# Moving small VectorE steps to GpSimd and ScalarE, and cutting the expert layer's inner units into blocks of 128, in a four-batch transformer kernel

## The reference, cut to what matters

```
x = x + tanh(g_xattn[0]) * L0_xattn(layernorm(x), ctx)    # autocorrelation attention by DFT
x = x + tanh(g_ffn[0])   * L0_ffn(layernorm(x))           # product-key memory
x = x + tanh(g_xattn[1]) * L1_xattn(layernorm(x), ctx)    # 16-head cross attention with rotary positions
x = x + tanh(g_ffn[1])   * L1_ffn(layernorm(x))           # 8 experts, routed
```

```
sx, ix = top_k(sim[0], 8);  sy, iy = top_k(sim[1], 8)
scores, pk = top_k(sx[..., :, None] + sy[..., None, :], 8)
h = softmax(scores) * gelu(x . down_embed[indices]);  out = sum(h * up_embed[indices])
```

```
for e in range(8):
    g = x @ gate_w[e].T ; u = x @ up_w[e].T          # 336 units
    y = (silu(g) * u) @ down_w[e].T ; out += scores[..., e] * y
```

## Time and profile before

| | us |
|---|---|
| median of 3 runs | 481.78 (481.11 to 484.6) |
| the profiled execution's own time | 483.82 |
| its span in the trace | 482.0 |
| PE busy / DVE busy / ACT busy / POOL busy | 393.0 / 331.5 / 202.2 / 124.6 |

### The profile page before, as it was taken

The page is one execution under the profiler, slowest core; times in us unless marked ns, Lnnn a source line. Parts: engine busy times, 40 slices in busy tenths (PEclk is TensorE's granted clock), DMA queues, the critical chain, the costliest instruction groups (busy, mean ns, idle before and its releaser), DMA issues. The chain is left out here.

```text
span 482.0 us, 8024 instructions
## 1 busy us (share of the span) xinstructions
PE 393.0 (82%) x2812; PEld 294.1 (61%) x2812; DVE 331.5 (69%) x1261; ACT 202.2 (42%) x435; POOL 124.6 (26%) x218
## 2 busy tenths in 40 slices
PE   8977699915525358786899899899999999999995
PEld 3866664305514235565576686678877675777784
DVE  7887557999999999989697838798522733132411
ACT  2343532711201004511374714247646387747542
POOL 2000101131023300220232255331242331352653
PEclk9989897975575655775695989999999999999999
DMA  7920000040000000000000000000000000000000
GB/s 221 413 105 0 1 1 2 1 114 1 1 1 1 1 0 1 2 0 2 0 1 2 2 0 1 1 0 13 1 1 2 0 2 13 1 0 1 11 2 12
DMA packets 5613, 11.29 MB, mean 23 GB/s; under 512 B 2004, under 2 KB 4180, under 8 KB 5077
## 3 DMA queue, kind: packets, MB, share of 16 engines
q1 hardware_dynamic: 5572, 10.79, 6.5%
HBM read 10.26 MB, written 0.52 MB: 22 GB/s over the span
## 5 line engine op out<-in xcount | busy, mean ns | idle before, releaser
L413 ACT ACTIVATE Sb<-ps 112x256 f32<-112x256 f32 (+2 forms) x90 | 40.3, 451 | 90.5 <-PE ps L1107 62.2
L384 POOL TENSOR_TENSOR Sb<-Sb 112x256 f32<-112x256 f32 x64 | 50.1, 789 | 108.3 <-ACT Sb L619 106.8
L1079 DVE SCALAR_TENSOR_TENSOR xnb<-ps,score,xnb 128x128 f32<-128x128 f32 x56 | 17.0, 346 | 64.3 <-PE ps L1107 64.1
L1107 PE MATMUL ps<-Y,Xb 128*128 128x32 f16 x512 | 40.0, 249 | 18.6 <-DVE Xb L937 14.7
L1107 PEld LDWEIGHTS ps<-Y,Xb 128*128 128x128 f16 x512 | 37.0, 164 | 26.6 <-DVE Xb L937 16.3
L1107 PEld LDWEIGHTS ps<-dnb,Sb 112*128 112x128 f32 x384 | 46.7, 192 | 9.8 <-issue 7.4
L1107 PE MATMUL ps<-dnb,Sb 112*128 112x128 f32 x384 | 49.5, 279 | 3.5 <-DVE xnb L1079 2.4
L1107 PE MATMUL ps<-ctxTb,sb_guT 128*112 128x256 f32 x192 | 51.1, 401 | 0.8 <-ACT ctxTb L413 0.6
L1107 PE MATMUL ps<-Xb,sb_guT 128*112 128x256 f32 x192 | 47.4, 386 | 0.0
L1019 DVE TENSOR_REDUCE mx<-ps 128x8 f32<-128x2048 f32 x16 | 36.6, 2286 | 9.5 <-PE ps L1107 9.2
L937 DVE TENSOR_TENSOR Xb<-sb_downT,iox 128x2048 f16<-128x2048 f16 x32 | 39.8, 1255 | 2.1 <-PE ps L1107 2.0
(11 more groups left out here) (263 smaller groups left out, 702.6 us busy)
## 6 DMA issues: line engine op xcount, KB each, us to landing
sb_guT<-in_guT SPq DMA_DIRECT2D x1, 2688.0 KB
dnb<-in_dn SPq DMA_DIRECT2D x1, 1344.0 KB
simb<-in_w_q SPq DMA_DIRECT2D x1, 1024.0 KB, 5.1
simb<-in_w_qT SPq DMA_DIRECT2D x1, 1024.0 KB, 7.2
Gb<-in_ctx SPq DMA_DIRECT2D x1, 512.0 KB, 4.0
Gb<-in_dft SPq DMA_DIRECT2D x1, 512.0 KB, 4.8
sb_x<-in_x SPq DMA_DIRECT2D x1, 512.0 KB
sb_downT<-in_downT SPq DMA_DIRECT2D x1, 512.0 KB, 8.1
```

Of the source, the lines that this page charges most:

```text
L384: g.tensor_tensor(av[:, m % 6, :], av[:, m % 6, :], up[m % 3], ALU.mult).then_inc(sem("av_ready"), 1)
L413: act.activation(dst, src, ACT.Copy, scale=scale).then_inc(sem(s), 1)
L1079: i = v.scalar_tensor_tensor(macc[:, t, :], y, w, macc[:, t, :], ALU.mult, ALU.add)
L1107: return pe.matmul(o, l, r, start=start, stop=stop)
```

## The change

1. **POOL takes the candidate sums.** For the six half-batches from batch 1 on, `pair` on DVE waits for `cand_ready` and does only the two best-of steps. A new POOL step `cands` does the four additions. `best` now raises `top_ready`, for which both wait.
2. **POOL takes `dd` and the cast.** A new POOL step `gap` subtracts the largest sum and casts `pk`, for the same six half-batches. `weight` waits for `pkf_ready`; `pkf` has two buffers.
3. **ACT scales the norms.** `norms1_b` and `norms3_b` leave DVE. ACT does them as x * r + nb, and POOL's root computes nb in three more links (two more operations in the chain and one beside it).
4. **The bias of `project` goes to POOL.** It is multiplied by the gate once (`bo1`), and a new POOL step `addb` adds it to x after the norm has read it (`xn2_ready`); `norms3` waits for `x2b_ready`. The two one-row matmuls of `project` are gone; those of `query` stay.
5. **`rope` takes both tiles at once:** 4 operations in place of 8.
6. **21 blocks of 128 units in place of 24 of 112.** The 8 x 336 units are one row of 2688. A block can belong to two experts, so `down` takes 3 or 4 blocks, 28 in all for eight experts in place of 24, with weights that are zero for the units of the other expert.
7. **All four lists of `ORDER` are new.**

```diff
-E8, I, IT, IP = 8, 336, 3, 112
+E8, I = 8, 336
+NB = E8 * I // P
...
+PIECE = [(e, n) for e in range(E8) for n in range(first(e), last(e) + 1)]
...
-onehots1.0 by_query0.0 by_query0.1 token1.0 by_query0.2 token1.1 by_query0.3 token1.2 token1.3 neg_max0.0 token1.4
+onehots1.0 turn_q0.0 by_query0.0 token1.0 by_query0.1 by_query0.2 token1.1 by_query0.3 token1.2 token1.3 token1.4
...
+            def cands(b, q):
+
+                t = 2 * b + q
+                g.wait_ge(sem("top_ready"), t + 1)
+                g.wait_ge(sem("pk_ready"), t - 1)
...
+            def gap(b, q):
+
+                t = 2 * b + q
+                g.wait_ge(sem("pk_ready"), t + 1)
+                g.wait_ge(sem("ex_ready"), t - 1)
+                g.tensor_tensor(dd[:, q, :, :], sc[:, q, :, :], sc[:, q, :, 0:1].broadcast_to([P, PH, 8]),
+                                ALU.subtract).then_inc(sem("dd_ready"), 1)
+                g.wait_ge(sem("hot_used"), t - 1)
+                g.tensor_copy(pkf[:, q, :].rearrange("p (k h) -> p h k", h=PH), pk[:, q, :, :]).then_inc(sem("pkf_ready"), 1)
...
+                g.tensor_tensor(x, x, ld["bo1"][:, :].unsqueeze(1).broadcast_to([P, 2, D]), ALU.add).then_inc(sem("x2b_ready"), 1)
...
+                    i = act.activation(dst[:, t, :], cur[:, 2 * b + t, :], ACT.Identity, bias=nb[:, at + t:at + t + 1],
+                                       scale=rs[:, 1, at + t:at + t + 1])
...
+                if t >= 2:
+                    v.wait_ge(sem("cand_ready"), t - 1)
+                    picked(q)
+                    return
...
+                if t >= 2:
+                    v.wait_ge(sem("pkf_ready"), t - 1)
...
-                    mm(o, attT[:, t * P:t * P + P], ld["Wo1"][:, :], True, False)
-                    i = bias(o, BO1, 128)
+                    i = mm(o, attT[:, t * P:t * P + P], ld["Wo1"][:, :])
...
-                    i = mm(ps[0:IP, m % 2, s * 256:s * 256 + 256], ld["guT"][:, e, s, k * IP:k * IP + IP], xn3T[b % 2])
+                    i = mm(ps[:, m % 2, s * 256:s * 256 + 256], ld["guT"][:, s, n * P:n * P + P], xn3T[b % 2])
...
-                    for k in range(IT):
-                        i = mm(ps[:, 2, t * D:t * D + D], av[:, (m * IT + k) % 6, t * P:t * P + P],
-                               ld["dn"][:, e * IT + k, :], k == 0, k == IT - 1)
+                    for n in range(first(e), last(e) + 1):
+                        i = mm(ps[:, 2, t * D:t * D + D], av[:, (b * NB + n) % 6, t * P:t * P + P],
+                               ld["dn"][:, PIECE.index((e, n)), :], n == first(e), n == last(e))
```

More of the change, by code:

```diff
@@ L26, with first, last, users @@
 CAND = 20
-E8, I, IT, IP = 8, 336, 3, 112
+E8, I = 8, 336
+NB = E8 * I // P
+def first(e):
+    return e * I // P
+def last(e):
+    return (e * I + I - 1) // P
+def users(n):
+    return min(E8 - 1, (P * n + P - 1) // I)
+PIECE = [(e, n) for e in range(E8) for n in range(first(e), last(e) + 1)]
 AH, MK = 50, 6
@@ L111 @@
+times3.13 times3.14 times3.15 times3.16 times3.17 times3.18 times3.19 times3.20
 """,
@@ L165, in program @@
                 shape = [P, 4]
-            if name == "bo":
+            if name in ("bo", "rows"):
                 continue
+            if name == "bo1":
+                shape = [P, D]
             if name == "dn":
-                dnb = sb("dnb", [P, E8 * IT * D])
-                ld[name] = dnb[0:IP, :].rearrange("p (a c) -> p a c", a=E8 * IT)
+                dnb = sb("dnb", [P, len(PIECE) * D])
+                ld[name] = dnb[:, :].rearrange("p (a c) -> p a c", a=len(PIECE))
             elif name in ("w_q", "w_qT"):
@@ L235, in program @@
         eidi = sb("eidi", [P, 3, P], I32)
+        ld["rows"] = hot[:, :, :].rearrange("p c j -> p (c j)").bitcast(F32)[0:1, 0:512]
         elh = sb("elh", [P, 2, P])
@@ L401, in norms3, with addb @@
                 root(2, b, "var3_ready", "root3_ready")
-            stages = {"look_a": look_a, "number": number, "times": times, "norms1": norms1, "norms3": norms3}
+            def addb(b, _):
+                x = cur[:, 2 * b:2 * b + 2, :]
+                g.wait_ge(sem("bo1_ready"), 1)
+                g.wait_ge(sem("xn2_ready"), b + 1)
+                g.tensor_tensor(x, x, ld["bo1"][:, :].unsqueeze(1).broadcast_to([P, 2, D]), ALU.add).then_inc(sem("x2b_ready"), 1)
+            stages = {"addb": addb, "look_a": look_a, "cands": cands, "gap": gap, "number": number, "times": times, "norms1": norms1, "norms3": norms3}
             look_a(0, 0)
@@ L561, in turn_2, with scaled, norms1_b, norms3_b @@
                 copy(xn2T[:, :], ps[:, 3, 0:256], "xn2T_ready")
+            def scaled(at, b, dst, root, used, signal):
+                act.wait_ge(sem(root), b + 1)
+                if b >= 1:
+                    act.wait_ge(sem(used), b)
+                for t in range(2):
+                    i = act.activation(dst[:, t, :], cur[:, 2 * b + t, :], ACT.Identity, bias=nb[:, at + t:at + t + 1],
+                                       scale=rs[:, 1, at + t:at + t + 1])
+                i.then_inc(sem(signal), 1)
+            def norms1_b(b, _):
+                scaled(0, b, xn2, "root2_ready", "xn2T_psum", "xn2_ready")
+            def norms3_b(b, _):
+                scaled(2, b, xn3, "root3_ready", "xn3T_psum", "xn3_ready")
             def turn_q(b, _):
@@ L1095, in _ @@
             stages = {"best": best, "where": where, "pair": pair, "weight": weight, "number": number,
-                      "groups": groups, "place": place, "weigh": weigh, "norms1": norms1, "norms3": norms3, "norms1_b": norms1_b, "norms3_b": norms3_b, "rope": rope,
+                      "groups": groups, "place": place, "weigh": weigh, "norms1": norms1, "norms3": norms3, "rope": rope,
                       "max": max_, "neg_max": neg_max, "attend": attend, "route2": route2, "rank": rank,
@@ L1107, in mm @@
                 return pe.matmul(o, l, r, start=start, stop=stop)
-            def bias(o, row, w):
-                return mm(o, ones[0:1, 0:P], ld["rows"][0:1, row:row + w], False, True)
-            BQ1, BKV1, BO1 = 384, 512, 768
             pe.wait_ge(sem("dc_clear"), 1)
@@ L1513, with pieces @@
     i = {k: np.asarray(v) for k, v in inputs.items()}
+    def pieces(w):
+        r = np.zeros((P, len(PIECE), D), np.float32)
+        for k, (e, n) in enumerate(PIECE):
+            h = np.arange(max(e * I, n * P), min(e * I + I, n * P + P))
+            r[h - n * P, k, :] = w[e][:, h - e * I].T
+        return r
     def tiles(x):
```

232 lines of the change are left out of this document (120 added, 112 removed).

## The result

The changed kernel takes 465.71 us (median of 4 runs, 464.99 to 467.78), the kernel before 482.78 on the same chip (4 runs). The ratio is 0.9653, 95% interval 0.9601 to 0.9704. Against those the gain is 15.2 (480.5 to 465.25 on one chip).

What follows compares the result with a forecast made beforehand. The time was taken as a stretch DVE sets plus one PE sets, joined at batch 2's `mix`. Terms -9.4 - 4.0 + 1.9 + 1.5 = -10.0 on 481.78 gave 471.8 us, own range 467 to 475.5, whole range 462 to 478.5.

Steps and rivals of the forecast that it cites:

- the first rival: More is won: waits go whole, denser matmuls keep the clock high, no contention; 465 us, chance 0.20.
- DVE ahead of the joint, -9.4: Before batch 2's `mix`, DVE saves 9.4 us on sums, casts, norm scaling, rope and two moved gathers.
- DVE's waits for PE, -4.0: Two DVE waits of 3.6 lose their cause in the new order; 4.0 taken between 0 and 7.2.
- PE behind the joint, +1.9: From batch 2's `mix` on: gates and downs +1.7, moved score and values +3.2, projects -3.0.
- the third rival: The blocks don't pay: a gate's rows go at the pace of their weights; 482 us, chance 0.04.
- DVE and POOL slow each other, +1.5: Before the joint, POOL's added work slows DVE by 1.5 us, between ends of 0 and 12.7.
- The fourth rival: DVE and POOL block each other, 12.7 us in place of 1.5; 483 us, chance 0.07.
- The second rival: PE at half clock takes over ahead of the joint; 475.5 us as middle, 477 at worst, chance 0.18.
- The fifth: Slower: POOL answers late and DVE stands at `pair` and `weight`, twelve waits of 1.69; 492 us, chance 0.05.
- the signs that were named: Batch 2's `mix` near 266, DVE some 15 less busy, PE over 94% busy behind, gate 0.92, POOL waits at most 2.

Runs made afterwards that it cites:

- the old order: All edits of the change, in the step order of the kernel before: 480.57 us, ratio to before 1.0007.
- no edit: The new order with the steps of the kernel before, 24 gate blocks and old engines: 489.59 us, ratio to before 1.0186.
- two gates: Changed kernel with gate0.0 and gate0.1 on TensorE again ahead of by_query1.1 and token2.1: 472.90 us, +7.7.
- one down: Changed kernel with down0.0 ahead of token2.6 on TensorE and gather0.0 right behind rank0.0 on VectorE: 477.21 us, +12.0.
- bias by TensorE: Changed kernel with the projection bias added by a ones-row product on TensorE again, without GpSimd's addition: 467.82 us, +2.6.
- pairs: Changed kernel with candidate sums, difference and cast of the picks back on VectorE for all pairs: 472.21 us, +7.0.
- scaling: Changed kernel with the scaling of the two inner norms back on VectorE: 471.96 us, +6.7.
- 24 blocks: Changed kernel with the inner units again in 24 blocks of 112, everything else as changed: 477.1 us, +11.8.
- the blocks alone: Kernel before with only the 21 blocks of 128 and the small routing tile moved to make room: 484.61 us, ratio 1.0088.

## Why the prediction came out as it did

The predicted 471.8 has the right sign, and 465.7 is inside the whole range (462 to 478.5), though below the forecast's own (467 to 475.5). The gain was 17.1 by the medians of the first chip, 16.0 by the two profiled executions and 15.2 on a later chip, and not 10.0. The mechanism, a stretch that DVE sets and one that PE sets, joined at the `mix` of batch 2, is right; three terms had the wrong size, all to the same side.

The number that came is that of the first rival (465), in part by luck. Its waits do go whole, and there is no contention that shows. But its up to 2 for a clock that stays high rested on the `mix` of 5.46, which takes 3.84 in the old order too, and what fills that place is DVE's own work, of which 2.1 more went than either had. Term by term:

- *DVE ahead of the joint, -9.4.* Measured -11.5. The edits' part was forecast at 8.1 and is 8.6 to 8.7, in both orders. The order's part was forecast at 1.3 (two gathers moved, 1.2 by the groups) and is 2.9 (184.18 to 181.27 with no edit); the rest is in many steps of the old work that take a little less each, why is open. A right term, undersized by a fifth.
- *DVE's waits for PE, -4.0.* This term was mis-sized: -6.9. The bounds were 0 and 7.2, and I took the middle for fear that waits would come back elsewhere. In the planned order one of 2.0 for ACT's copy does, but smaller ones that the term left out went as well (1.4 to 0.2 at the norm, and 0.9 for GpSimd's root). The runs showed the fear to be right for the other orders tried: moving two gates brought 5.2 of idle time back, one down 9.0, the old order 9.4. The price of a wait should have been taken from the new order itself. There a single gate at half clock (235.88, 2.04 for 4 rows) stands ahead of a `by_query` and a token step that DVE needs next, where before there were two, and no wait of DVE follows it; the 0.7 is at the last `max`, behind two gates at full clock.
- *PE behind the joint, +1.9.* Measured +2.4 in busy time and +0.8 in length, as idle time fell by 1.6, which the sum did not ask about. Gates were forecast at 119.3 to 121.0 with the downs; the groups give 132.3 and 134.2, both higher than by start-to-start but with the same difference of about 2 (gates -8.4, downs +10.3, for -8.3 and +10.0). A project of four rows takes 0.48 to 0.52 at full clock, and with the bias by TensorE 1.6: 1.1 each and not 1.0. The gate at 128 columns costs 0.90, so the third rival's mechanism, rows at the pace of their weights, is out. That the blocks are worth little by themselves is shown for the old order; in the new one they are worth 5.4 of TensorE's time behind the joint.
- *DVE and POOL slow each other, +1.5.* Nothing measurable: with 12.2 us more of the same work VectorE is busy 0.3 less. The fourth rival is out for these steps; of the rule in the Trainium skill (SBUF — State Buffer, section on the two separate sides), by which the loser of the shared pair blocks for the whole instruction, this run shows no cost. The run does not say that nothing slows VectorE: the products of `groups` still take 795 to 828 ns in the mean where the fastest take 683.
- *The second rival* (PE at half clock takes over ahead of the joint) did not happen here, but its mechanism is what makes the order with two gates early slow: they take 3.75 us at half clock. With one down ahead it is the loop of waits around the `gather`, and the clock falls within it.
- *The fifth* did not happen: no wait for GpSimd in the list. With the edits in the old order one of 1.6 appeared.

Of the signs that were named, the `mix` starts earlier than forecast (261.3 for 266), DVE's busy time is 16.8 less in all (for some 15), PE is 94.5% busy from the joint on (for over 94%), and a gate's four rows take 0.90 (for 0.92).

What failed as a method is the sum itself. It adds parts that do not add: undone one at a time from the changed kernel, pairs, scaling, bias, blocks and order give 7.0 + 6.7 + 2.6 + 11.8 + 15.3 = 43.4, where the whole is 15 to 17. Each undoing also breaks an order that was planned for the durations that it changes. My expectations for single runs, made by that sum, missed upward six times (two gates +7.7 for 2.0 to 3.7, one down +12.0 for 0.5 to 2, 24 blocks +11.8 for 4 to 6, order alone 489.6 for 478 to 483, edits in the old order 480.6 for 470 to 474, and the blocks alone +4.6 for -2.5 to -4).

Open: how much of each loss is clock and how much is the wait that set it off, since no run held the clock while it moved a step.
